# All steps of the block quantization on one engine: the pattern QPAT set from (0, 1, 1, 1, 1, 1, 1, 1) to (1,)

## The chip, the cores and the metric

The kernel runs as one program on the 8 cores of one Trainium2 chip. Each core takes 1024 of the 8192 tokens and works by itself; no data passes between cores. The metric is the device time of the slowest core in microseconds (us). A profile shows one execution on the slowest of its cores; here that is core 5.

The engines are called as in the profile: PE (TensorE, matmul), PEld (its weight load), DVE (VectorE), ACT (ScalarE), POOL (GpSimd), SP (the queue that issues DMAs here).

## The reference, cut to what matters

One transformer layer: linear attention with a memory, a layer norm, and then a feed-forward block whose inputs and weights are quantized in blocks of 32 (a shared power of two per block, and few mantissa bits per element), and a second layer norm. H is 2048, I is 8192.

```python
def _quantize_mx(x, ebits, mfrac, emax_elem, max_norm):
    xb = x.reshape(shp[:-1] + (shp[-1] // BLOCK, BLOCK))
    amax = jnp.max(jnp.abs(xb), axis=-1, keepdims=True)
    sexp = jnp.floor(jnp.log2(jnp.where(amax == 0, 1.0, amax))) - emax_elem
    scale = jnp.exp2(sexp)
    q = _quantize_elem(xb / scale, ebits, mfrac, max_norm) * scale
...
gate = _mx_linear(x, w_gate)
up = _mx_linear(x, w_up)
inter = jax.nn.silu(gate) * up
return _mx_linear(inter, w_down)
```

`_mx_linear` quantizes both operands and multiplies them. The kernel quantizes the float32 weights itself, on every core.

## The kernel before

**Stages.** After the attention (to about 410 us of the span) comes stage C: a layer norm and the quantization of the activations, eight tiles of 128x2048. Then the feed-forward runs over 16 slabs s of 512 columns of I, and a last layer norm ends the kernel.

**Quantizations.** `emit_quant` (L234) is one quantization; outside stage C its tile is 128x1024. It has three parts, and the names are used below.
- *Head*: the product with the inverse scale (L252, `tt`) and the clamp (L254, `ts`), on engine `se`.
- *Middle*: the square on ACT (L255), and then three DVE instructions that build the magic number from it (L256, L257, L259), on DVE whatever `se` is.
- *Tail*: add, subtract and the product with the scale into the bf16 output (L269 to L271), again on `se`, and then `post`, the transposing DMAs issued by SP.

The tail isn't emitted with its own head. It is kept in `tmp["pend"]` and emitted within the next quantization, after that one's head and middle (L263), or by `flushq`. Each engine works in the order in which things were emitted. So an engine that holds consecutive quantizations has the order head q0, (tail of the one before), head q1, tail q0, head q2, tail q1 and so on.

**Which engine.** A counter `QC` runs over all 456 quantizations (8 in stage C, 448 in the slabs). `se` is DVE where `QPAT[k % 8]` is 0, which is every eighth, and POOL elsewhere. The work buffers of the two engines are apart (fy0, fmd0, fmd1 for DVE; fy1, fmd2, fmd3 for POOL). POOL's quantizations alternate over `par`: with `par` 1 the tile y is the borrowed region `yb`, which for weights is `INTER[:, 1024:2048]` and for the intermediate is `WST[:, 1024:2048]` (key `wst0b`).

**A weight job.** `wq_back` (L566) quantizes one pair of staged weight tiles: `emit_search` on DVE (a memset, 15 short chained instructions, a reciprocal that writes `invw`), then four quantizations q0 to q3, each 128x1024. After q1 and after q3 it calls `wq_load_tile` for the next job (L601): two DMAs from ACT's queue into the half of WST just read, and a `tensor_reduce` on DVE for the block maxima. All four quantizations write the one buffer WQN, which a transposing DMA empties each time.

**A slab.** For s above 0 the order is: job d1 of slab s-1 (the second half of w_down), g0 and g1 (w_gate), u0 and u1 (w_up), `down_section(s-1)` (its matmuls and 32 adds to BIG2 on DVE), then four times two gate/up tiles with silu and one quantization of the intermediate (i0 to i3), each with its own search that writes `invi`, and then d0. Pending tails are flushed before the down section, before each of i0 to i3 and before d0. d0's weights are loaded only after i3, since nothing else was in the pipe.

**Where DVE quantizations fall.** A slab has 28 quantizations and the pattern has 8, so it repeats every two slabs. In odd slabs q0 of d1, g1, u1 and d0 is on DVE. In even slabs q0 of g0 and u0, and i0, are on DVE. It is always the first quantization of its job. No two jobs that follow one another without a break are both without a DVE quantization.

Of the kernel before, what the change touches and what calls it, by code (L numbers as in the profile page):

```python
# [161 lines left out]
def build_program():  # L162
# [20 lines left out]
    with ExitStack() as stG:  # L183
# [40 lines left out]
            p.recip(qi_ap, q_ap, [kq], [kqi])  # L224

        QC = [0]
        QPAT = (0, 1, 1, 1, 1, 1, 1, 1)

        def flushq(tmp):
            if tmp["pend"] is not None:  # L230
# [3 lines left out]
        def emit_quant(src_ap, src_keys, inv_bc, scale_tile_ap, blk0, scale_keys,  # L234
                       out_ap, out_keys, kc_col, hi, tmp, tasp, post=()):
            k = QC[0]
            QC[0] += 1
            se = "gp" if QPAT[k % len(QPAT)] else "dve"
            par = tmp["p" + se]
# [536 lines left out]
```

How the kernel before makes its waits and increments, by code:

```python
        def go(h, _w=tuple(waits), _b=build, _hs=hsem, _inc=inc):  # L90
            for hs, v in _w:
                h.wait_ge(hs, v)
            ins = _b(h)
            if _hs is not None:
                ins.then_inc(_hs, _inc)
# [9 lines left out]
    def wait_raw(self, eng, sem, val):  # L105
        hs = self.semh[sem]
        self.ops[eng].append(lambda h, _hs=hs, _v=val: h.wait_ge(_hs, _v))
```

## Time and profile before

| | us |
|---|---|
| median of 2 runs (7924.15 to 7967.17) | 7945.66 |
| the profiled execution | 7966.37 |
| its span on core 5, the slowest | 7964.8 |
| spans of the 8 cores | 7908.4 to 7964.8 |

The profiled execution is 0.26% above the median. All eight cores do the same work within 0.7% of each other. A row of the trace below has the start and the duration in us, the engine, the line, the operation, the tile written and the tiles read, the count, and in square brackets how long the engine had been idle and what ended it. L122, L126, L127, L130, L136, L139 and L144 are the helpers `tt`, `ts` with one scalar, `ts` with two, `stt`, `recip`, `red` and `act`. A reciprocal that writes invw or invi ends a search, so these 160 reciprocals mark the jobs; the stretch from one to the next is called the interval of the job.

### The profile page before, as it was taken

How to read it: one execution, taken by the hardware profiler on the slowest of the kernel's cores; microseconds unless marked ns; L12 is line 12 of the kernel's file. 1: busy time of each engine (PE TensorE's matmuls, PEld its weight loads, DVE VectorE, ACT ScalarE, POOL GpSimd, SP SyncE). 2: the span in 40 equal slices, each digit the busy share in tenths (PEclk: the TensorE clock that was granted, in tenths of full speed). 3: DMA queues.
4: the chain of work that ended last, by engine and by line, in shares of the span. 5: the costliest groups of instructions: out<-in, count | busy, mean ns of one | idle time of the engine just before them, and what ended most of it. 6: DMA issues, size and time to landing. Idle time of an engine off the chain costs nothing.

```text
span 7964.8 us, 37328 instructions; the slowest of 8 cores (7908.4 to 7964.8 us)
## 1 busy us (share of the span) xinstructions
PE 1627.1 (20%) x6816; PEld 712.1 (9%) x6816; DVE 5351.7 (67%) x6206; ACT 596.4 (7%) x634; POOL 4341.0 (55%) x2015
## 2 busy tenths in 40 slices
PE   4400202104040402104040402104040402104041
PEld 2100101001010101001010101001010100001010
DVE  3386666676767666676767666676767667676767
ACT  0010000000000000000000000000000000000001
POOL 0037565574747465574747465574747465564643
PEclk7555656557575756557575756557575756657575
DMA  3001121111212021111212021111212121111111
GB/s 107 0 8 53 27 60 37 53 46 38 57 28 58 24 61 37 48 51 34 62 28 57 25 61 37 48 50 35 61 26 60 25 59 39 48 50 34 56 29 63
DMA packets 670364, 355.00 MB, mean 45 GB/s; under 512 B 499121, under 2 KB 630578, under 8 KB 668978
## 3 DMA queue, kind: packets, MB, share of 16 engines
q10 hardware_dynamic: 169984, 201.35, 8.2%
q1 hardware_dynamic: 496818, 134.49, 7.5%
q0 software_dynamic: 3328, 16.78, 0.6%
q14 instruction: 177, 1.45, 0.1%
q8 instruction: 57, 0.93, 0.0%
HBM read 222.50 MB, written 8.39 MB: 29 GB/s over the span
## 4 chain that ended last, share of the span: by engine, by line
DVE 38%; POOL 27%; issue 13%; PE 10%; DMA 7%; ACT 3%; DVEq 1%; ACTq 1%; POOLq 0%; SPq 0%
POOL fy L122 9%; POOL INTER L122 8%; PE psY L148 7%; DVE s_c L130 7%; POOL WQN L122 5%; DVE fmd L127 4%; DVE fy L122 4%; DVE PSC L139 3%; DVE INTER L127 3%; DMA WST<-wd 3%; DVE scw L122 3%; ACT fmd L144 2%; DVE fmd L130 2%; DVE WQN L122 2%; DVE sci L122 2%
## 5 line engine op out<-in xcount | busy, mean ns | idle before, releaser
L148 PE MATMUL psY<-WDT,INTQF 128*128 128x512 bf16 x2048 | 519.0, 421 | 5445.5 <-DVE BIG L122 2911.8
L127 DVE TENSOR_SCALAR INTER<-fmd 128x1024 f32<-128x1024 f32 x384 | 555.8, 1447 | 1028.0 <-ACT fmd L144 1022.0
L122 POOL TENSOR_TENSOR fy<-fy,fmd 128x1024 f32<-128x1024 f32 x392 | 989.3, 2524 | 328.7 <-DVE fmd L130 290.7
L122 POOL TENSOR_TENSOR INTER<-INTER,fmd 128x1024 f32<-128x1024 f32 x336 | 858.1, 2554 | 200.7 <-DVE fmd L130 167.1
L130 DVE SCALAR_TENSOR_TENSOR fmd<-INTER,smalls,fmd 128x1024 f32<-128x1024 f32 x384 | 891.8, 2322 | 43.8 <-DVE fmd L127 2.3
L127 DVE TENSOR_SCALAR fmd<-fmd,smalls 128x1024 f32<-128x1024 f32 x448 | 806.8, 1801 | 49.1 <-DVE INTER L127 0.9
L148 PEld LDWEIGHTS psY<-WDT,INTQF 128*128 128x128 bf16 x2048 | 215.3, 106 | 5749.3 <-issue 5556.3
L122 POOL TENSOR_TENSOR fy<-WST,invw 128x1024 f32<-128x1024 f32 x168 | 412.5, 2455 | 552.3 <-DVE invw L136 536.6
L122 POOL TENSOR_TENSOR INTER<-WST,invw 128x1024 f32<-128x1024 f32 x168 | 412.5, 2455 | 500.6 <-DVE invw L136 484.9
L139 DVE TENSOR_REDUCE PSC<-WST 128x64 f32<-128x2048 f32 x192 | 438.3, 2283 | 222.4 <-DMA WST<-wd 197.8
L144 ACT ACTIVATE fmd<-fy 128x1024 f32<-128x1024 f32 x252 | 263.8, 1056 | 3611.7 <-POOL fy L127 2269.0
L148 PE MATMUL psG<-WGT,XQF 128*128 128x512 bf16 x1024 | 406.5, 397 | 414.0 <-DVE scw L122 397.9
L148 PE MATMUL psU<-WUT,XQF 128*128 128x512 bf16 x1024 | 407.1, 398 | 187.9 <-DMA WUT<-WQN 108.4
L122 POOL TENSOR_TENSOR WQN<-INTER,scw 128x1024 bf16<-128x1024 f32 x168 | 361.5, 2152 | 121.7 <-DMA WGT<-WQN 33.7
L122 POOL TENSOR_TENSOR WQN<-fy,scw 128x1024 bf16<-128x1024 f32 x168 | 361.5, 2152 | 121.4 <-DMA WGT<-WQN 33.6
L122 DVE TENSOR_TENSOR BIG<-BIG,psY 128x512 f32<-128x512 f32 x512 | 350.0, 687 | 114.6 <-PE psY L148 101.4
L148 PE MATMUL psY<-WGT,XQF 128*128 128x512 bf16 x1024 | 388.1, 379 | 0.0
L148 PE MATMUL psY<-WUT,XQF 128*128 128x512 bf16 x1024 | 388.1, 379 | 0.0
L122 POOL TENSOR_TENSOR WST<-INTER,invi 128x1024 f32<-128x1024 f32 x28 | 53.5, 1911 | 502.5 <-DVE invi L136 502.5
L122 POOL TENSOR_TENSOR fy<-INTER,invi 128x1024 f32<-128x1024 f32 x28 | 53.5, 1911 | 486.0 <-DVE invi L136 486.0
L144 ACT ACTIVATE fmd<-INTER 128x1024 f32<-128x1024 f32 x168 | 177.3, 1055 | 1825.6 <-POOL INTER L127 1825.6
L122 DVE TENSOR_TENSOR scw<-scw,s_c 128x128 f32<-128x128 f32 x480 | 204.8, 427 | 50.7 <-DVE s_c L130 1.2
(170 smaller groups left out, 3895.8 us busy)
## 6 DMA issues: line engine op xcount, KB each, us to landing
WST<-wg ACTq DMA_DIRECT2D x128, 512.0 KB, 4.6
WST<-wu ACTq DMA_DIRECT2D x128, 512.0 KB, 4.7
WST<-wd ACTq DMA_DIRECT2D x128, 512.0 KB, 6.0
xps<-xP POOLq DMA_DIRECT2D x8, 1024.0 KB, 7.0
BIG<-xT SPq DMA_DIRECT2D x16, 512.0 KB, 19.2
y<-BIG POOLq DMA_DIRECT2D x8, 1024.0 KB, 4.2
WGT<-WQN SPq DMA_TRANSPOSE x128, 2.8
WUT<-WQN SPq DMA_TRANSPOSE x128, 2.8
```

What stands on the lines that cost most here:

```text
L122: return self.emit(eng, lambda h: h.tensor_tensor(out, a, b, op), reads, writes)
L127: return self.emit(eng, lambda h: h.tensor_scalar(out, a, s1, s2, op1, op2), reads, writes)
L130: return self.emit(eng, lambda h: h.scalar_tensor_tensor(out, a, s, b, op1, op2), reads, writes)
L139: return self.emit("dve", lambda h: h.tensor_reduce(out, a, AX, op, apply_absolute_value=absval), reads, writes)
L144: return self.emit("act", lambda h: h.activation(out, a, func, bias=bias, scale=scale), reads, writes)
L148: return self.emit("pe", lambda h: h.matmul(out, lhsT, rhs, start=start, stop=stop), reads, writes, quiet=quiet)
```

## The change

The pattern has one entry, 1. `se` is then POOL for all 456 quantizations.

```diff
@@ -224,7 +224,7 @@
         QC = [0]
-        QPAT = (0, 1, 1, 1, 1, 1, 1, 1)
+        QPAT = (1,)
```

What follows in the code: 57 quantizations (one in stage C, 48 of weights, 8 of the intermediate) have head and tail on POOL instead of DVE; their middle stays on DVE and ACT. `par` then alternates over all quantizations, so that i0 and i2 always use the tile fy1 and i1 and i3 always the region `WST[:, 1024:2048]`. No instruction and no DMA is added or removed.

## Rows read from the trace of the kernel before

**Rows 1.** The page, part 1: busy us (share of the span) xinstructions.

```profile
span 7964.8 us, 37328 instructions; the slowest of 8 cores (7908.4 to 7964.8 us)
...
PE 1627.1 (20%) x6816; PEld 712.1 (9%) x6816; DVE 5351.7 (67%) x6206; ACT 596.4 (7%) x634; POOL 4341.0 (55%) x2015
```

**Rows 2.** Instructions by line: xcount | busy us, mean ns | idle before, releasers.

```profile
L122 POOL TENSOR_TENSOR fy<-fy,fmd 128x1024 f32<-128x1024 f32 x392 | 989.3, 2524 | 328.7 <-DVE fmd L130 290.7 <-POOL fy L122 1.3
...
L122 POOL TENSOR_TENSOR WQN<-fy,scw 128x1024 bf16<-128x1024 f32 x168 | 361.5, 2152 | 121.4 <-DMA WGT<-WQN 33.6 <-DMA WDT<-WQN 33.5 <-DMA WUT<-WQN 16.9
...
L122 DVE TENSOR_TENSOR fy<-fy,fmd 128x1024 f32<-128x1024 f32 x112 | 230.1, 2055 | 7.0 <-DVE fy L122 0.5
...
L122 DVE TENSOR_TENSOR WQN<-fy,scw 128x1024 bf16<-128x1024 f32 x48 | 149.3, 3111 | 8.0 <-DVE fy L122 7.1
...
L122 DVE TENSOR_TENSOR fy<-WST,invw 128x1024 f32<-128x1024 f32 x48 | 58.8, 1226 | 5.0
```

**Rows 3.** Busy time by stretch: jobs g1, u0 of slab 1.

```profile
core 5: us, PE busy (x) PEld busy (x) DVE busy (x) ACT busy (x) POOL busy (x), PEclk, DMA share, GB/s
...
1187.73:1236.57 48.84, 0.00 (x0) 0.00 (x0) 39.92 (x38) 4.12 (x4) 26.95 (x12) 0.50 0.20 59
...
1236.57:1296.35 59.78, 0.00 (x0) 0.00 (x0) 41.77 (x33) 4.23 (x4) 49.26 (x23) 0.50 0.21 57
```

**Rows 4.** Sums of that view over 32, 31, 8, 8, 8, 7, 8, 8 intervals.

```profile
sum 1565.32, PE 25.19 PEld 7.96 DVE 1276.66 ACT 131.83 POOL 860.99; mean PE 0.79 PEld 0.25 DVE 39.90 ACT 4.12 POOL 26.91
...
sum 1855.53, PE 65.03 PEld 23.05 DVE 1293.86 ACT 131.11 POOL 1525.84; mean PE 2.10 PEld 0.74 DVE 41.74 ACT 4.23 POOL 49.22
...
sum 390.79, PE 0.00 PEld 0.00 DVE 319.01 ACT 32.95 POOL 215.54; mean PE 0.00 PEld 0.00 DVE 39.88 ACT 4.12 POOL 26.94
...
sum 431.37, PE 0.00 PEld 0.00 DVE 303.23 ACT 33.84 POOL 334.63; mean PE 0.00 PEld 0.00 DVE 37.90 ACT 4.23 POOL 41.83
...
sum 694.99, PE 381.13 PEld 169.47 DVE 454.87 ACT 42.51 POOL 258.49; mean PE 47.64 PEld 21.18 DVE 56.86 ACT 5.31 POOL 32.31
...
sum 674.15, PE 336.88 PEld 149.39 DVE 398.45 ACT 37.97 POOL 344.94; mean PE 48.13 PEld 21.34 DVE 56.92 ACT 5.42 POOL 49.28
...
sum 237.20, PE 0.00 PEld 0.00 DVE 101.81 ACT 8.46 POOL 76.26; mean PE 0.00 PEld 0.00 DVE 12.73 ACT 1.06 POOL 9.53
...
sum 271.35, PE 0.00 PEld 0.00 DVE 101.80 ACT 8.46 POOL 76.27; mean PE 0.00 PEld 0.00 DVE 12.72 ACT 1.06 POOL 9.53
```

**Rows 5.** Timeline: start us, us. From g0's search to g1's in slab 1.

```profile
1118.65 2.28 DVE L139 TENSOR_REDUCE PSC<-WST 128x64 f32<-128x2048 f32 x1
...
1127.95 0.95 DVE L136 RECIPROCAL invw<-scw 128x128 f32<-128x128 f32 x1
...
1129.11 1.91 POOL L122 TENSOR_TENSOR fy<-WST,invw 128x1024 f32<-128x1024 f32 x1 [11.46 <-DVE invw L136]
...
1132.30 5.09 POOL L122 TENSOR_TENSOR INTER<-INTER,fmd 128x1024 f32<-128x1024 f32 x2
...
1175.31 2.28 DVE L139 TENSOR_REDUCE PSC<-WST 128x64 f32<-128x2048 f32 x1
...
1175.53 4.83 POOL L122 TENSOR_TENSOR INTER<-INTER,fmd 128x1024 f32<-128x1024 f32 x2 [1.23 <-DVE fmd L130]
...
1180.62 1.95 DVE L122 TENSOR_TENSOR scw<-scw,s_c 128x128 f32<-128x128 f32 x1
...
1187.73 0.95 DVE L136 RECIPROCAL invw<-scw 128x128 f32<-128x128 f32 x1
```

**Rows 6.** Timeline: after i3 in slab 1 (first two) and slab 3.

```profile
1452.90 1.91 POOL L122 TENSOR_TENSOR INTQ<-WST,sci 128x1024 bf16<-128x1024 f32 x1
...
1460.12 2.29 DVE L139 TENSOR_REDUCE PSC<-WST 128x64 f32<-128x2048 f32 x1 [12.38 <-DMA WST<-wd]
...
2356.27 2.29 DVE L139 TENSOR_REDUCE PSC<-WST 128x64 f32<-128x2048 f32 x1 [7.24 <-DMA WST<-wd]
```

**Rows 7.** Busy time by stretch: one quantization of stage C.

```profile
596.27:618.57 22.30, 0.00 (x0) 0.00 (x0) 14.37 (x4) 1.91 (x1) 21.62 (x6) 0.50 0.10 24
```

## The prediction

> **What bounds the kernel now.** I read the page first, for the shares. DVE is busy 67% of the span, POOL 55%, PE 20% [rows 1]. No engine is near full, so shares can't say what a change is worth; the reader should see only that the two engines between which work moves are the busiest two, and that neither is saturated. So I looked for what ends each job. The timeline of one job shows it [rows 5]: a search writes invw at 1127.95, POOL had been idle 11.46 us and starts at once, and the next search ends at 1187.73. This is a loop. Search, heads and tails on POOL, the middle of q3 on DVE, the block maximum of the next tile (the reduce at 1175.31), search. Each turn waits for the one before, so a job's interval is a piece of the kernel's path, and the time is the sum of intervals plus the attention and the end, which the change doesn't touch.
>
> Next, the busy time by stretch, over one interval of each kind [rows 3]. A job whose q0 is on DVE (DVE-led) takes 48.84 us, one with all four on POOL (all-POOL) takes 59.78. DVE is busy about as long in both (39.92 and 41.77), POOL 26.95 and 49.26. The kernel before thus contains both kinds of every job, and the change turns all of them into the second kind. The sums of that view over all intervals give the prices [rows 4], in the order of the eight rows:
> - 32 DVE-led intervals of d1, g0, g1, u0: 1565.32, mean 48.92. 31 all-POOL ones: 1855.53, mean 59.86.
> - d0, 8 and 8: 390.79 (mean 48.85) and 431.37 (mean 53.92).
> - u1, up to the first search of the intermediate, so with the down section: 8 DVE-led, 694.99 (86.87); 7 all-POOL with a down section, 674.15 (96.31).
> - i3, up to the search of d0: 8 on the tile fy1, 237.20 (29.65); 8 on the region in WST, 271.35 (33.92).
>
> **The change part by part.**
>
> *The moved tail is paid on the path.* On DVE the two adds and the product of a tail take 2 x 2.055 + 3.111 = 7.2 us, on POOL 2 x 2.524 + 2.152 = 7.2 us [rows 2]. So the work isn't dearer on POOL. The matter is where it lies. With q0 on DVE both engines make a head at once and both make tails at once; with q0 on POOL the heads and tails stand in one line between invw and q3's middle. That is the 59.86 - 48.92 = 10.94 us of the two means [rows 4].
>
> *But not all of that stays.* An all-POOL interval in the kernel before is always followed by a DVE-led job (or by a flush). The tail of its q3 is emitted within the next q0, and where this q0 is on DVE no POOL head comes before it. POOL then runs that tail at 1175.53, just as DVE reduces and searches. The search is stretched: a tensor_tensor of 128x128 takes 1.95 us in it [rows 5]. How much, its length tells. From the start of the last reduce to invw it is 1187.73 - 1175.31 = 12.42 us here and 1127.95 - 1118.65 = 9.30 us at the end of the DVE-led job before, where POOL was idle (the 11.46) [rows 5]. The difference is 3.12 us. After the change a POOL head stands ahead of that tail and waits for invw; the tail comes after the search, as at 1132.30, where an all-POOL job already has it and where it is in its 59.86. So an all-POOL job followed by another costs 59.86 - 3.12 = 56.74 us. That isn't shown by any interval of before as a whole; it is put together from two halves that are. Its bounds are 59.86 (nothing saved) and 59.86 - 3.12 - 0.4 (some jobs are 0.35 longer than others, from 59.78 to 60.14, and this could go too).
>
> The Trainium skill has a rule for this stretch (SBUF — State Buffer, "Who interferes with whom"): GpSimd and VectorE share one pair of ports as an exclusive lock, held for a whole instruction, and a VectorE instruction with two SBUF inputs needs it. The stretched tensor_tensor is of that kind, so the trace agrees. By the rule the sum is the one below; without it, if the 3.12 us had another cause, it is that of the first rival.
>
> *The sum over weight jobs.* d1, g0, g1, u0: 63 x 56.74 = 3574.6 against 1565.32 + 1855.53 = 3420.9: +153.7. d0: its all-POOL form has no pending tail at its start and ends in the same stretched search: 53.92 - 3.12 = 50.80, 16 times 812.8 against 822.2: -9.4. u1 is followed by a flush, so its q3 tail stays where it is and nothing is saved: 8 x (96.31 - 86.87) = +75.5. The final d1 is all-POOL already: 0.
>
> *The intermediate.* Eight i0 move to POOL. i0's interval doesn't change by more than 0.2 us between the two kinds; POOL is otherwise idle there. I take 0, with a price of the 10.9 us of a quantization each, 8 x 10.9 = 87 us, if that cover were gone. But the alternation `par` shifts: i3 is then always on the region in WST. There its last instruction on POOL runs from 1452.90, and d0's weights can be loaded into that half of WST only after it, so DVE's reduce waits 12.38 us for the DMA; with the tile fy1 it waits 7.24 [rows 6]. Eight slabs change over: 8 x (33.92 - 29.65) = +34.2. Those are means of eight intervals each [rows 4].
>
> *Stage C.* A steady quantization takes 22.30 us, POOL busy for 21.62 of it [rows 7]. One more on POOL costs at most 22.3. It costs less, since the DVE one ran beside POOL's first one, under contention, and held back POOL's second. Laying the eight out in POOL's order with the steady 22.3 gives about 7. Bounds 0 and 22.3; I take 7, because POOL's idle time at the start of the stage closes.
>
> *DMAs and queues.* No transfer is added. SP's transposes follow each tail as before. WQN, one buffer for all tails, is written every 11.5 us in the all-POOL stretch and was written there at the same pace before.
>
> Sum: 153.7 - 9.4 + 75.5 + 34.2 + 0 + 7 = +261 us. Against the profiled execution's own 7966.4 us that is 8227, +3.3%. That execution is 0.26% above the median of the runs shown; from the median 7945.7 it is 8207 us. That is the forecast.
>
> **The rivals.**
> *A. Nothing is saved.* The stretch of the search is replaced by another of the same size, for instance by q2's tail, if that slips behind the reduce. Then 3.12 us come back 63 + 16 times, +246, in all +507: 8453 us. For it: only the halves were seen. Against: q2's tail ended before the reduce in the DVE-led job, POOL idle for 11.46 us [rows 5].
> *B. DVE is the bound, faster.* DVE is the busiest engine [rows 1], and the change takes 57 heads and tails off it. The Trainium skill says that with VectorE saturated, offloading even to GpSimd may make sense, and in the same place that it might not help, as the two share a port (Perfetto Trace Analysis, "Optimizing Scalar/DVE Operations"). If DVE's work set the time, the tails (7.2 us) and the first product of a head (1.23) [rows 2] would leave: 57 x 8.4 = 479, 7467 us. This decides only if an interval follows DVE's busy time. It doesn't: DVE is busy 1.8 us more in a job that is 10.9 us longer [rows 3], because its instructions stretch beside POOL's.
> *C. Hidden, no change.* POOL is idle 48.84 - 26.95 = 21.9 us in a DVE-led job, and the moved quantization needs 22.3 more (49.26 - 26.95) [rows 3]. If it all fell into that idle time, all jobs would take 48.9 and the change be worth 0 to the old DVE-led jobs: 7946 plus the 41 of i3 and stage C, 7987 us. Against it stand the 31 all-POOL jobs, which have just that load and take 59.86 [rows 4].
>
> **How the numbers follow.** Forecast 0.86, A 0.07, C 0.04, B 0.03. The forecast's own range: without i3's term and with 0.4 us less in 63 jobs it is 8207 - 34 - 25 = 8148; with stage C at 22.3 and half a microsecond more in 79 jobs 8207 + 15 + 40 = 8262, and the runs of before differ by 43 us among themselves. I give 8150 to 8280. It leaves out the rivals, 14 in 100, and a few at its edges. A measurement of this kernel can tell about 2% from no change, 159 us, or 8105 us. The forecast and A are slower by more; C and a thin tail of the forecast are within; B is faster: 0.92, 0.05, 0.03.
>
> **What would show it.** POOL has 57 x 5 = 285 instructions more, 2300, and DVE 285 fewer, 5921. Intervals between invw are near 56.7 for d1, g0, g1, u0, near 50.8 for d0, 96.3 for u1. No 1.95 us tensor_tensor is left in the weights' searches, and 9.3 us lie between the last reduce and invw. i3's interval is near 33.9 in all 16 slabs. DVE's busy time falls by little, some 200 to 300 us, and not by 479. The forecast is wrong if these intervals are 59.8 (A), 49 (C), or if two all-POOL jobs in a row make a wait that none of these halves has, such as the load of the next tile coming late for its reduce.

## The result: 3.2% slower

| | us |
|---|---|
| before, median of 10 runs (7920.26 to 7969.31) | 7956.09 |
| changed, median of 11 runs (8190.33 to 8223.35) | 8194.4 |
| ratio, 95% interval | 1.0322 [1.0300, 1.0344] |
| forecast | 8207 (8150 to 8280) |
| span of the profiled execution, before and changed | 7964.8 and 8190.1 |

**The profile after.** Its part 1, and the first line of the chain that ended last (part 4):

```profile
span 8190.1 us, 37698 instructions; the slowest of 8 cores (8175.6 to 8190.1 us)
...
PE 1628.2 (20%) x6816; PEld 711.8 (9%) x6816; DVE 5110.6 (62%) x5921; ACT 601.1 (7%) x634; POOL 4872.8 (59%) x2300
...
POOL 43%; DVE 26%; issue 14%; PE 10%; DMA 3%; ACT 3%; DVEq 1%; POOLq 1%; ACTq 0%; SPq 0%
```

Against [rows 1], POOL has 285 instructions more and DVE 285 fewer, as counted in the forecast. DVE gives back only 241 us of busy time for them, POOL takes 532 us more, and the span grows by 225. The chain runs over POOL for 43% of the span; before it was DVE that led:

```profile
DVE 38%; POOL 27%; issue 13%; PE 10%; DMA 7%; ACT 3%; DVEq 1%; ACTq 1%; POOLq 0%; SPq 0%
```

The intervals between searches say where the time went. First one weight job, u0 of slab 1 (busy time by stretch; the columns are those of [rows 3]):

```profile
1267.67:1324.28 56.61, 0.00 (x0) 0.00 (x0) 38.60 (x33) 4.23 (x4) 42.67 (x20) 0.50 0.20 56
```

Where [rows 3] had 48.84 and 59.78, all such jobs now take about 56.6 us. The sums of the view, in the order of the four kinds of [rows 4]: 63 intervals of d1, g0, g1, u0; 16 of d0; the 15 of u1 that hold a down section; 16 of i3.

```profile
sum 3566.07, PE 88.24 PEld 30.60 DVE 2424.70 ACT 266.36 POOL 2678.33; mean PE 1.40 PEld 0.49 DVE 38.49 ACT 4.23 POOL 42.51
...
sum 811.60, PE 0.00 PEld 0.00 DVE 557.59 ACT 67.64 POOL 563.33; mean PE 0.00 PEld 0.00 DVE 34.85 ACT 4.23 POOL 35.21
...
sum 1437.74, PE 714.97 PEld 317.50 DVE 854.63 ACT 81.33 POOL 738.90; mean PE 47.66 PEld 21.17 DVE 56.98 ACT 5.42 POOL 49.26
...
sum 517.25, PE 0.00 PEld 0.00 DVE 203.56 ACT 16.90 POOL 152.54; mean PE 0.00 PEld 0.00 DVE 12.72 ACT 1.06 POOL 9.53
```

| intervals | before | forecast | changed, mean | difference in the sum, forecast / found |
|---|---|---|---|---|
| d1, g0, g1, u0 (63) | 48.92 and 59.86 | 56.74 | 56.60 | +153.7 / +145.2 |
| d0 (16) | 48.85 and 53.92 | 50.80 | 50.73 | -9.4 / -10.6 |
| u1 (16, one without a down section) | 86.87 and 96.31 | 96.31 | 95.85 | +75.5 / +70.0 |
| i0, i1, i2 (48) | | no change | 18.95 | 0 / 0 |
| i3 (16) | 29.65 and 33.92 | 33.92 | 32.33 | +34.2 / +8.6 |
| up to the first weight search | | | | +7 / +11.0 |
| the last down section and layer norm | | 0 | | 0 / +0.8 |

The last column adds up to +261 forecast and +225 found between the two profiled spans. (The found +70.0 of u1 counts its first interval too, 79.96 and 81.37 us.) Only i3 is far from its term. Why it is, the last experiments show.

Now the piece that no interval of before had shown as a whole, the search between two all-POOL jobs. Timeline of the end of that job and the start of the next: POOL, then DVE.

```profile
1306.63 5.09 POOL L122 TENSOR_TENSOR fy<-fy,fmd 128x1024 f32<-128x1024 f32 x2
...
1311.87 2.17 POOL L122 TENSOR_TENSOR WQN<-fy,scw 128x1024 bf16<-128x1024 f32 x1
...
1325.44 1.91 POOL L122 TENSOR_TENSOR fy<-WST,invw 128x1024 f32<-128x1024 f32 x1 [11.40 <-DVE invw L136]
...
1315.04 2.28 DVE L139 TENSOR_REDUCE PSC<-WST 128x64 f32<-128x2048 f32 x1
...
1318.42 0.29 DVE L130 SCALAR_TENSOR_TENSOR s_c<-s_c,scw 128x128 f32<-128x128 f32 x1
...
1318.82 0.29 DVE L122 TENSOR_TENSOR scw<-scw,s_c 128x128 f32<-128x128 f32 x1
...
1324.28 0.95 DVE L136 RECIPROCAL invw<-scw 128x128 f32<-128x128 f32 x1
```

POOL finishes the tail of q2 at 1314.04 (1311.87 + 2.17) and then has nothing that doesn't need invw: it is idle 11.40 us. So the reduce at 1315.04 and the whole search have no POOL instruction beside them. The two search instructions shown take 0.29 us, where [rows 5] had 1.95 for the second of them, and from the reduce to invw it is 1324.28 - 1315.04 = 9.24 us (9.30 was put in, 12.42 is the stretched form).

### The profile page after: what moved, and what is told of

It is laid out like the page before. It is cut to its first block, busy times and chain, and to the rows that moved or that the text cites. A ratio compares the mean times of both kernels' runs of the same rounds, so it can differ in the third digit from the quotient of the medians.

```text
span 8190.1 us, 37698 instructions; the slowest of 8 cores (8175.6 to 8190.1 us)
## 1 busy us (share of the span) xinstructions
PE 1628.2 (20%) x6816; PEld 711.8 (9%) x6816; DVE 5110.6 (62%) x5921; ACT 601.1 (7%) x634; POOL 4872.8 (59%) x2300
## 4 chain that ended last, share of the span: by engine, by line
POOL 43%; DVE 26%; issue 14%; PE 10%; DMA 3%; ACT 3%; DVEq 1%; POOLq 1%; ACTq 0%; SPq 0%
POOL INTER L122 17%; POOL fy L122 12%; POOL WQN L122 7%; PE psY L148 7%; DVE s_c L130 6%; DVE fmd L127 4%; DVE PSC L139 3%; ACT fmd L144 2%; DVE INTER L127 2%; DVE sci L122 2%; DVE scw L122 2%; POOL fy L127 2%; POOL WST L122 2%; DMA WST<-wd 2%; POOL INTER L127 1%
## 5 line engine op out<-in xcount | busy, mean ns | idle before, releaser
L127 DVE TENSOR_SCALAR INTER<-fmd 128x1024 f32<-128x1024 f32 x384 | 615.5, 1603 | 1466.3 <-ACT fmd L144 1464.1
L122 POOL TENSOR_TENSOR fy<-fy,fmd 128x1024 f32<-128x1024 f32 x448 | 1107.5, 2472 | 225.2 <-DVE fmd L130 178.4
L127 DVE TENSOR_SCALAR fmd<-fmd,smalls 128x1024 f32<-128x1024 f32 x448 | 1037.5, 2316 | 50.2 <-DVE INTER L127 2.3
L130 DVE SCALAR_TENSOR_TENSOR fmd<-INTER,smalls,fmd 128x1024 f32<-128x1024 f32 x384 | 1033.2, 2691 | 43.0 <-DVE fmd L127 1.4
L122 POOL TENSOR_TENSOR INTER<-INTER,fmd 128x1024 f32<-128x1024 f32 x384 | 945.0, 2461 | 63.0 <-DVE fmd L130 20.8
L122 POOL TENSOR_TENSOR INTER<-WST,invw 128x1024 f32<-128x1024 f32 x192 | 505.5, 2633 | 27.0 <-POOL WQN L122 0.9
L144 ACT ACTIVATE fmd<-fy 128x1024 f32<-128x1024 f32 x224 | 236.7, 1057 | 3710.0 <-POOL fy L127 3710.0
L122 POOL TENSOR_TENSOR WQN<-fy,scw 128x1024 bf16<-128x1024 f32 x192 | 425.4, 2216 | 28.1 <-POOL fy L122 0.9
L122 POOL TENSOR_TENSOR WQN<-INTER,scw 128x1024 bf16<-128x1024 f32 x192 | 412.4, 2148 | 28.1 <-POOL INTER L122 0.9
L127 POOL TENSOR_SCALAR fy<-fy 128x1024 f32<-128x1024 f32 x224 | 232.8, 1039 | 36.5 <-POOL fy L122 36.5
```

The costliest lines, as they stand in the source:

```text
L122: return self.emit(eng, lambda h: h.tensor_tensor(out, a, b, op), reads, writes)
L127: return self.emit(eng, lambda h: h.tensor_scalar(out, a, s1, s2, op1, op2), reads, writes)
L130: return self.emit(eng, lambda h: h.scalar_tensor_tensor(out, a, s, b, op1, op2), reads, writes)
L144: return self.emit("act", lambda h: h.activation(out, a, func, bias=bias, scale=scale), reads, writes)
```

## The experiments

Each is compared with the kernel before on the same chip; the ratios are those of runs to runs of before. The kernel before took 7927.7 us on the chip of the first four experiments and 7931.5 on that of the next four (medians of 7), against 7956.1 above, so a difference in us between two sections is uncertain by some 30 us; the intervals are not. The intervals are read as above, on the slowest core of each run.

### Does i3's load wait for the tile? Yes

The edit swaps the two tiles for the intermediate; `W`, the width, is only computed further up (those lines are left out here).

```diff
...
-            if se == "gp" and par == 1 and yb is not None:
+            if se == "gp" and par == (0 if kc_col == 6 and W == 1024 else 1) and yb is not None:
                 y, kys = yb, list(yb_keys)
             else:
-                y, kys = tmp["y"][se], [ky + str(par if se == "gp" else 0)]
+                y, kys = tmp["y"][se], [ky + "0"]
```

> The changed kernel, with the two work tiles swapped for the intermediate: i1 and i3 use the tile fy1, i0 and i2 the region WST[:, 1024:2048]. Theory (d0's load waits for i3's last POOL instruction because that one reads the half of WST to be loaded): the 16 intervals of i3, 32.3 us in the changed kernel, go to the 29.7 that slabs with the tile fy1 had in the kernel before, so 16 x 2.6 = 42 us less than the changed kernel's 8194, about 8152, and DVE's first wait for the wd load there falls from 11.9 to about 7.2 us. Rival (the wait is the transfer itself, whatever the tile): i3 stays at 32.3 and the time at 8194.

Measured 8111.6 us, ratio 1.0223 [1.0199, 1.0247]: 1.0 point below the changed kernel's 1.0322, about 80 us, of which the 16 i3 intervals hold 86 (517.25 - 430.81). First the changed kernel after i3 of slab 1 (timeline: POOL's last instruction of i3, DVE's reduce), then DVE's reduce after i3 of slab 7 in this run, and the sum over its 16 i3 intervals:

```profile
1489.75 1.91 POOL L122 TENSOR_TENSOR INTQ<-WST,sci 128x1024 bf16<-128x1024 f32 x1
...
1496.44 2.29 DVE L139 TENSOR_REDUCE PSC<-WST 128x64 f32<-128x2048 f32 x1 [11.86 <-DMA WST<-wd]
```

```profile
4236.82 2.29 DVE L139 TENSOR_REDUCE PSC<-WST 128x64 f32<-128x2048 f32 x1 [6.03 <-DMA WST<-wd]
...
sum 430.81, PE 0.00 PEld 0.00 DVE 203.62 ACT 16.90 POOL 152.56; mean PE 0.00 PEld 0.00 DVE 12.73 ACT 1.06 POOL 9.53
```

The mechanism holds: with i3 on fy1 the wait falls from about 12 us to 5.7 to 6.7 in 12 of the 16 slabs (7.1 to 8.5 in slabs 0 to 3), and the interval from 32.33 to 26.93. The size was expected at half of what it is: the expectation took 29.65 for the tile fy1 from [rows 4], and it is 26.93 here. The last experiments say why.

### Same work, another order: the loop sets the time

```diff
                     if nxt is not None:
+                        if idx == 1:
+                            flushq(tmpw)
                         wq_load_tile(nxt[0], nxt[1], nxt[2] + idx, nxt[3])
```

> The changed kernel (all on POOL), with the tail of q3 emitted at the end of its own job, ahead of the next job's first head, instead of behind it. The work of each engine stays the same, to the instruction. Theory (the loop from invw to invw sets the time, and a search with a POOL tail beside it is stretched by 3.1 us): a job then has no pending tail at its start but a stretched search at its end, the form that d0 had in the kernel before, 53.9 us. So 63 intervals of d1, g0, g1, u0 go from 56.7 to 53.9 (-176), 16 of d0 from 50.7 to 53.9 (+51), 15 of u1 from 95.9 to about 90 (-89): about 7980 us. Rival (POOL's total work, or its rate, sets the time, not the place of its work): no change, 8194.

Measured 7999.5 us, ratio 1.0084 [1.0060, 1.0107], 195 us less than the changed kernel with the same number of instructions on every engine. The sum of the 63 job intervals, and the end of one job (POOL's tail of q3, DVE's reduce and invw):

```profile
sum 3398.52, PE 93.17 PEld 31.44 DVE 2394.28 ACT 266.34 POOL 2633.01; mean PE 1.48 PEld 0.50 DVE 38.00 ACT 4.23 POOL 41.79
...
2143.76 4.83 POOL L122 TENSOR_TENSOR INTER<-INTER,fmd 128x1024 f32<-128x1024 f32 x2 [1.23 <-DVE fmd L130]
...
2143.53 2.28 DVE L139 TENSOR_REDUCE PSC<-WST 128x64 f32<-128x2048 f32 x1
...
2155.95 0.95 DVE L136 RECIPROCAL invw<-scw 128x128 f32<-128x128 f32 x1
```

The mean is 3398.52 / 63 = 53.94 us, the expected form. POOL's tail of q3 lies beside the search again, and from reduce to invw it is 2155.95 - 2143.53 = 12.42 us, the stretched length to the hundredth. It pays all the same: 3.1 us of stretch against 5.9 us (59.86 - 53.92 of [rows 4]) of tail that no longer stands between invw and q3. POOL's amount of work doesn't set the time; what stands in the loop does. The 20 us over the expectation are i3 again: 34.16 us on the profiled core and its neighbour, 32.2 on the six others, whose spans are 7963 to 7971 us against 7997 and 7998.

### The same split between the engines, another place

```diff
-        QPAT = (0, 1, 1, 1, 1, 1, 1, 1)
+        QPAT = (1, 1, 1, 0, 1, 1, 1, 1)
```

> The kernel before with the one DVE quantization in eight put last in its job (q3) instead of first: pattern (1,1,1,0,1,1,1,1). The split of the work between DVE and POOL is that of the kernel before. Rival (the balance of work between the two engines decides): 7956 as before. Theory (the place in the loop decides): a DVE q3 takes head and middle in DVE's own queue, behind the middle of q2, so the search begins hardly earlier; its tail delays the next job's q1 and the buffer WQN. I expect intervals of about 55 to 56 us for both kinds of job instead of 48.9 and 59.9, mean 1.1 more than before, about 8030 us (7990 to 8080).

Measured 8015.7 us, ratio 1.0104 [1.0081, 1.0128]: slower than before with the same split of the work. The sum over the 63 intervals, and DVE in one job whose q3 it holds (invw, head, last instruction of the middle, reduce):

```profile
sum 3472.80, PE 84.38 PEld 29.37 DVE 2475.75 ACT 266.34 POOL 2359.20; mean PE 1.34 PEld 0.47 DVE 39.30 ACT 4.23 POOL 37.45
...
2097.85 0.95 DVE L136 RECIPROCAL invw<-scw 128x128 f32<-128x128 f32 x1
...
2133.68 1.21 DVE L122 TENSOR_TENSOR fy<-WST,invw 128x1024 f32<-128x1024 f32 x1
...
2142.81 1.28 DVE L130 SCALAR_TENSOR_TENSOR fmd<-INTER,smalls,fmd 128x1024 f32<-128x1024 f32 x1
...
2144.01 2.29 DVE L139 TENSOR_REDUCE PSC<-WST 128x64 f32<-128x2048 f32 x1
```

The mean is 55.12 us against 54.30 in the kernel before (3420.9 / 63), and the intervals are near 54.8 and 55.4, not 48.9 and 59.9. DVE begins q3's head only behind q2's middle (2133.68), so the reduce stands at the same distance from invw as in an all-POOL job, within 2 us (2144.01 - 2097.85 = 46.2; 47.4 in [rows 5]). The expectation had the place right and the size within 15 us. Not all of the kernel follows it: on the slowest core u1 takes 82 us more in all than in the kernel before and i3 69 us less (part of that a disturbance of i3 in before, see the last experiments), which nearly cancel.

### The opposite of the change

```diff
-        QPAT = (0, 1, 1, 1, 1, 1, 1, 1)
+        QPAT = (0, 1, 1, 1)
```

> The opposite of the change: pattern (0,1,1,1), q0 of every weight job (and of every i0, and two of stage C) on DVE. Theory: each DVE-led job is now followed by another, whose q3 tail runs beside the search, so its interval is 48.9 + 3.1 = 52.0 us: 63 x 52.0 against 63 x 56.7 in the changed kernel (-296), d0 52.0 against 50.7 (+20), u1 86.9 against 95.9 (-144), stage C and i3 about -30 together: about 7740 us, 2.7% faster than the kernel before. Rival (DVE is the scarce engine, and the kernel before had the best split): 7956 or slower. Rival 2 (contention for the shared port grows with more on both engines): intervals well above 52.

Measured 7714.9 us, ratio 0.9728 [0.9701, 0.9756], faster than both kernels. Sum of the 63 intervals, and one search (DVE; then the POOL tail beside it):

```profile
sum 3282.23, PE 84.57 PEld 30.13 DVE 2710.61 ACT 259.34 POOL 2111.53; mean PE 1.34 PEld 0.48 DVE 43.03 ACT 4.12 POOL 33.52
...
1153.29 2.28 DVE L139 TENSOR_REDUCE PSC<-WST 128x64 f32<-128x2048 f32 x1
...
1156.27 0.29 DVE L130 SCALAR_TENSOR_TENSOR s_c<-scw,PSC 128x128 f32<-128x128 f32 x1
...
1156.67 1.82 DVE L130 SCALAR_TENSOR_TENSOR s_c<-s_c,scw 128x128 f32<-128x128 f32 x1
...
1158.59 1.95 DVE L122 TENSOR_TENSOR scw<-scw,s_c 128x128 f32<-128x128 f32 x1
...
1166.06 0.95 DVE L136 RECIPROCAL invw<-scw 128x128 f32<-128x128 f32 x1
...
1153.51 4.83 POOL L122 TENSOR_TENSOR INTER<-INTER,fmd 128x1024 f32<-128x1024 f32 x2 [1.23 <-DVE fmd L130]
```

The mean is 52.10 us. DVE is busier than in any kernel so far, 43.0 of those 52 us, and the time falls: the rival that DVE is the scarce engine (B of the forecast) is out. What is added to the 48.9 is the stretch of the search, 1.82 and 1.95 us for two instructions while POOL's tail runs, 1166.06 - 1153.29 = 12.77 us from reduce to invw. The instruction just before them, beside the same tail, has one input in SBUF (scw) and one in PSUM, writes the same SBUF tile, and takes 0.29 us; none of the 480 of its kind exceeds 0.29 us in this trace or in that of before.

### What stretches the search

```diff
-            s_c2 = sf("s_c2", [128, 128])
...
-            PSC = pf("PSC", [128, 160])
+            PSC = pf("PSC", [128, 288])
+            s_c2 = PSC[:, 160:288]
...
```

The same edit on the changed kernel (the control, where no POOL work lies beside the weights' searches) and on the kernel with every job DVE-led.

> The changed kernel with one edit: the searches' scratch s_c2 lies in PSUM (behind PSC, in the same bank) instead of SBUF, so that none of the 15 search instructions has two SBUF inputs. This is the control for the next run. Theory (a search instruction with two SBUF inputs waits for POOL's): in the weights' searches of the changed kernel nothing is stretched, so its intervals of 56.7, 50.7 and 95.9 stay; the searches of i1, i2, i3 do have POOL's tail beside them (1.5 and 1.95 us instead of 0.19) and lose up to 3.1 us each, 48 of them, less what PE then bounds: 8194 - 70 to 150, about 8090 us. A price of PSUM access would show as longer instructions in the weights' searches; the ones that read PSC take 0.29 us as the others do, so I expect none. Rival (the stretch has another cause): 8194 and i1 to i3 still 18.9.

> Every job DVE-led (pattern (0,1,1,1)), and the searches' scratch in PSUM. Here POOL's q3 tail lies beside every weight search. Theory: the 3.1 us of each go, 52.0 becomes 48.9: 63 + 16 times 3.1 = -245, and i1 to i3 another -70 to -150 as in the control: 7715 - 245 - 100 = about 7370 us. Rival (the stretch is no matter of the second SBUF input): 7715 less only what the control shows.

The control measured 8062.9 us, ratio 1.0163 [1.0139, 1.0186]. Its 63 job intervals, and its 48 of i0, i1, i2:

```profile
sum 3569.04, PE 88.07 PEld 30.49 DVE 2427.15 ACT 266.51 POOL 2677.77; mean PE 1.40 PEld 0.48 DVE 38.53 ACT 4.23 POOL 42.50
...
sum 764.45, PE 551.93 PEld 242.19 DVE 433.88 ACT 102.76 POOL 458.78; mean PE 11.50 PEld 5.05 DVE 9.04 ACT 2.14 POOL 9.56
```

The weights' intervals stay (56.65, were 56.60), and those of the intermediate go from 18.95 to 15.93 us. The DVE-led kernel measured 7385.8 us, ratio 0.9304 [0.9283, 0.9325]. Its 63 intervals, and a search with the POOL tail beside it:

```profile
sum 3086.95, PE 88.26 PEld 30.57 DVE 2515.18 ACT 259.34 POOL 2108.82; mean PE 1.40 PEld 0.49 DVE 39.92 ACT 4.12 POOL 33.47
...
1135.79 2.28 DVE L139 TENSOR_REDUCE PSC<-WST 128x64 f32<-128x2048 f32 x1
...
1139.18 0.30 DVE L130 SCALAR_TENSOR_TENSOR PSC<-PSC,scw 128x128 f32<-128x128 f32 x1
...
1139.58 0.29 DVE L122 TENSOR_TENSOR scw<-scw,PSC 128x128 f32<-128x128 f32 x1
...
1145.44 0.95 DVE L136 RECIPROCAL invw<-scw 128x128 f32<-128x128 f32 x1
...
1136.01 4.83 POOL L122 TENSOR_TENSOR INTER<-INTER,fmd 128x1024 f32<-128x1024 f32 x2 [1.23 <-DVE fmd L130]
```

The mean is 49.00 us instead of 52.10. The tail on POOL runs as before, right beside, and the same two instructions take 0.30 and 0.29 us. So the stretch needs two things at once, POOL instructions beside the search and search instructions whose two inputs both lie in SBUF; taking away either one removes it. The edit also moves the scratch that those instructions write, but writing to SBUF is not what stretches: `s_c<-scw,PSC` of the section before writes there and stays at 0.29 us. The Trainium skill says that a VectorE instruction with two SBUF inputs contends with a GpSimd instruction that reads SBUF, and one with at most one SBUF input, outside the 2-port perf modes, does not (SBUF — State Buffer, "Who interferes with whom"); both halves agree with these traces. Writing to PSUM costs 0.01 us per instruction.

### All together, and the other side of the optimum

The first: weight jobs DVE-led, i0 to i3 on POOL with i1 and i3 on fy1, scratch in PSUM. The part of the edit that chooses the engine (the tiles and the scratch are changed as above):

```diff
...
-            QC[0] += 1
-            se = "gp" if QPAT[k % len(QPAT)] else "dve"
+            if not (kc_col == 6 and W == 1024):
+                QC[0] += 1
+            se = "dve" if k % 4 == 0 and not (kc_col == 6 and W == 1024) else "gp"
```

> All together: weight jobs DVE-led, all of i0 to i3 on POOL with i1 and i3 on the tile fy1, the searches' scratch in PSUM. Theory: against the run before, i3 goes from a mean of 29.3 (half of the slabs near 32, half near 26.4) to 26.4 in all slabs, -46 us, and i0 stays: about 7320 us. Rival (an i0 on POOL without other cover costs its 10.9 us): 7320 + 175.

Measured 7282.3 us, ratio 0.9176 [0.9156, 0.9196], 8% less than the kernel before. Its 16 i3 intervals sum to

```profile
sum 427.84, PE 0.00 PEld 0.00 DVE 204.49 ACT 16.90 POOL 152.54; mean PE 0.00 PEld 0.00 DVE 12.78 ACT 1.06 POOL 9.53
```

26.74 us each. It is 38 us better than expected because i0 on POOL doesn't just cost nothing: with the search no longer stretched an i0 on POOL takes 15.97 us and one on DVE 18.85 (the run before). The rival's 10.9 us each are out.

The second keeps the searches as they were and puts two quantizations of each job on DVE, `QPAT = (0, 1, 0, 1)`.

> Pattern (0,1,0,1): q0 and q2 of each job on DVE, searches as in the kernel before. One more head and tail go from POOL to DVE. Theory: in a DVE-led job DVE is already busy 40 of 49 to 52 us, and five more instructions of 10.4 us in all don't fit: DVE becomes the engine that sets the interval, 54 to 58 us: about 8000 us (7850 to 8150), so the other side of the optimum. Rival (the more that runs side by side the better, POOL being the slow one): intervals below 52 and a time below 7715.

Measured 7757.0 us, ratio 0.9790 [0.9751, 0.9830]. The 63 intervals:

```profile
sum 3268.17, PE 88.28 PEld 30.63 DVE 2860.28 ACT 259.49 POOL 1529.56; mean PE 1.40 PEld 0.49 DVE 45.40 ACT 4.12 POOL 24.28
```

51.88 us, no more than with one (52.10). My expectation of 54 to 58 was wrong: DVE's other instructions get shorter as POOL has less to run beside them (the three of the middle from 18.7 to 11.9 us a job in all), so DVE is busy only 2.4 us longer (45.4). The rival had the direction right by 0.2 us and the time wrong: the kernel as a whole is 42 us slower than with one, by u1 (+26) and by i3 (+50), less 34 in other places. i3's tile is the WST region in every slab with this pattern. With none, one in eight, one in four and one in two on DVE the kernel takes 8194, 7956, 7715 and 7757 us.

### Why i3's term was off

Two more runs, one execution each. The first is the changed kernel with w_down loaded in long rows; it loads another piece of w_down of the same size, so its product is another one. (The lines that issue the two DMAs change with it and are left out here.) The second is the kernel before, unchanged.

```diff
-                    srcap = wd.rearrange("(c p) i -> p c i", p=128)[
-                        :, :, s * ISLAB + ti * 128: s * ISLAB + (ti + 1) * 128]
+                    n4 = s * NQT + ti
+                    srcap = wd[(n4 // 4) * 128:(n4 // 4 + 1) * 128,
+                               (n4 % 4) * 2048:(n4 % 4 + 1) * 2048]
...
```

> The changed kernel with w_down's tiles loaded in rows of 4 KB (a different piece of w_down of the same size) instead of in pieces of 512 bytes; the product with w_down is then of the wrong weights, all work stays the same. Theory (what differs between cores in i3 is the landing of the load in small pieces, which a neighbour core's load at the same moment slows): the load lands like that of w_gate and w_up (4.4 instead of 4.9 us), i3 goes from 32.1 us to about 31, and cores whose pair starts i3 within 2 us of them show no 34. Rival (any load is slowed by a neighbour's, or the pieces don't matter): 32.1, and 34 where a pair is close.

> The kernel before, unchanged, for a second trace of it. Theory (two cores of a pair, 0 and 1, 2 and 3, 4 and 5, 6 and 7, slow each other's w_down load when they reach i3 within 2 us of each other): every pair with a larger offset has i3 at 26.2 (tile fy1) and 32.0 (region in WST) and 7058 to 7066 us between the first and the last weight search; a pair that is closer has 29.6 and 34.0 and about 45 us more. Rival (cores 4 and 5 are slower by themselves): they have 29.6 and 34.0 whatever their offset.

Measured 8222.9 and 7936.6 us. Of the first only the i3 intervals on core 4 are used: cores 0 to 3 took 8181 to 8221 us at a granted clock of 0.586 to 0.589, cores 4 to 7 took 8162 to 8171 at 0.595 to 0.596.

All eight cores are in each trace. The times of a core count from its own first instruction, and no view has a clock common to two cores. So the distances below, between the starts of the i3 intervals of two cores, take it that a pair starts together; that they sort the intervals as they do speaks for it. In the profiled execution of before, cores 4 and 5 reached i3 within 2 us of one another in every slab; the other pairs were 3 to 12 us apart. The sums of eight i3 intervals each, on fy1 and on the WST region, on core 0 of that same execution, against 237.20 and 271.35 on core 5 in [rows 4]:

```profile
sum 208.99, PE 0.00 PEld 0.00 DVE 101.78 ACT 8.45 POOL 76.32; mean PE 0.00 PEld 0.00 DVE 12.72 ACT 1.06 POOL 9.54
...
sum 255.93, PE 0.00 PEld 0.00 DVE 101.77 ACT 8.45 POOL 76.32; mean PE 0.00 PEld 0.00 DVE 12.72 ACT 1.06 POOL 9.54
```

26.1 and 32.0 us, against 29.65 and 33.92. From the first to the last weight search it is 7056 to 7066 us on six cores, and 7109 and 7110 on cores 4 and 5. In the second trace of before, core 5 was 5 to 9 us from core 4, and its sums are

```profile
sum 207.54, PE 0.00 PEld 0.00 DVE 101.81 ACT 8.45 POOL 76.27; mean PE 0.00 PEld 0.00 DVE 12.73 ACT 1.06 POOL 9.53
...
sum 256.40, PE 0.00 PEld 0.00 DVE 101.78 ACT 8.45 POOL 76.27; mean PE 0.00 PEld 0.00 DVE 12.72 ACT 1.06 POOL 9.53
```

with 7061 us from first to last search: nothing is slow about core 5 itself. There cores 2 and 3 were 0.7 to 1.4 us apart in slabs 0 to 4 and 4 to 7 us from slab 5 on. Their i3 took 28.6 to 31.2 and 34.0 to 34.6 us in the first five slabs and 25.7 to 26.7 and 31.9 to 32.8 in the rest; from first to last search 7078 and 7081. Over nine of the traces (before, changed, and all runs but the one with q3 on DVE and the last two), four pairs and 16 slabs each:

| distance of the pair at i3, us | i3 on fy1: count, mean | i3 on the WST region: count, mean |
|---|---|---|
| under 1 | 10, 30.7 | 6, 35.2 |
| 1 to 2 | 16, 29.3 | 74, 34.2 |
| 2 to 3 | 12, 28.2 | 8, 33.6 |
| 3 to 4 | 18, 27.5 | 68, 32.4 |
| 4 and more | 392, 26.2 | 548, 32.2 |

The rival of a slow core falls. The spans of executions without a kept trace show the pairs too. Of the 12 executions of the changed kernel with all spans on record, 7 took 8190 to 8194 us; in each of the 5 that took 8216 to 8223, both cores of one or two pairs took 8214 to 8222 and all others 8194 or less. In the kernel before, in each of the 6 of 17 that took over 7940 us, the two longest cores (in one of them the four longest) are whole pairs. What is not shown is the cause as such: no run sets the distance on purpose, so "close together" and "long i3" are seen to go together and to end together, and no more.

The forecast's i3 term took both its numbers from a disturbed core and was set against a changed kernel whose pairs were all 3.5 us or more apart. From the first to the last weight search all its cores take 7317 to 7324 us, 251 to 268 more than the six. In i3 alone the rise between undisturbed cores is 16 x 32.2 - 208.99 - 255.93 = +50 us, and between the profiled ones +8.6 (517.25 - 508.55), since in the profiled execution of the changed kernel no pair was close. With w_down in long rows the loads land in 4.3 us instead of 4.9 (medians over the kernel; 6.0 on core 5 of before), and the 16 i3 intervals on core 4 are

```profile
sum 502.84, PE 0.00 PEld 0.00 DVE 203.61 ACT 16.90 POOL 152.53; mean PE 0.00 PEld 0.00 DVE 12.73 ACT 1.06 POOL 9.53
```

31.43 us instead of 32.2: the small pieces cost 0.8 us of an undisturbed i3. No pair came within 2 us in this run, so whether long rows would end the disturbance is open, and so is what the two cores share. The Trainium skill says that the two cores of a domain share the HBM's bandwidth (HBM Reference, "Specifications (TRN2)"); that fits pairs 0 and 1, 2 and 3 and so on, and no run here tells it from another shared part.

## Why the prediction was right, step by step

- **What bounds the kernel.** The loop from invw to invw: right. Moving one tail out of it, with no change in work, gave 195 us; DVE at its highest share gave a faster kernel.
- **The search unstretched, 3.12 us.** Right, and it was the step that mattered. The 59.86 us of the all-POOL jobs of before became 56.60; taking the long form over as it stood would have given rival A's 8453. The cause of the stretch was shown apart, by the scratch in PSUM on the DVE-led kernel.
- **d1, g0, g1, u0: +153.7, found +145.2.** The mean of 62 of them is 56.70. What I missed is slab 0's g0: it has no pending tail and takes 50.69, as d0 does, so 6 us of the 8.5.
- **d0: -9.4, found -10.6; u1: +75.5, found +70.0.** Right. u1's intervals alternate between about 95.4 and 96.5 us in the changed kernel, which is not explained.
- **i0 at nothing: right. i3: +34.2, found +8.6.** The mechanism is right; the term was mis-sized, since both rows it was read from held 2 to 3.5 us that go with a neighbour close by. Between undisturbed cores it is +50. The sign given for it, 33.9 us in all 16 slabs, failed: it is 32.33. The step that failed is reading a price off one core without looking at the others: the spans of before, 7908 to 7965 us for the same work, were the sign, and [rows 4] was read on the slowest of them.
- **Stage C: +7, found +8.1.** From the reciprocal before the stage to the first weight search, before and changed (busy time by stretch):

```profile
503.32:701.30 197.98, 0.00 (x0) 0.00 (x0) 132.33 (x50) 15.18 (x8) 153.63 (x35) 0.50 0.13 32
...
506.21:712.28 206.07, 0.00 (x0) 0.00 (x0) 119.85 (x45) 15.28 (x8) 168.66 (x40) 0.50 0.12 31
```

  The other 2.9 us came before the stage, in the attention, which the change doesn't touch.
- **What would show it.** 2300 and 5921 instructions, DVE's busy time down by 241 us (200 to 300 was said), no long search instruction, 9.24 us from reduce to invw: as written. i3's interval was not, as said.
- **The rivals.** A (8453), B (7467) and C (7987) are each out by more than 200 us. C's idle time on POOL is real, 11.40 us in the job shown of the changed kernel, and the moved work can't use it, because the head that would fill it needs invw. The flush puts a tail there, and gains.

The forecast of 8207 was 13 us over the median. Part of that is luck. Against the profiled spans i3 was 25 us too high and the jobs 15, stage C and the attention 4 too low. Between the executions that by their times no pair disturbs (before, the four of ten at 7920 to 7926 us; changed, the six of eleven at 8190 to 8194) the change costs 268 us, near the +261 of the sum, with i3 16 us too low there. But the starting point, 7946, lay between such executions and disturbed ones, and so does the median of before, 7956, while the changed kernel's 8194 does not: the medians differ by 238.

## What to carry to other kernels

Where two engines take turns around a dependent loop, as here, neither's busy share prices a move between them. Find the event that closes the loop, take the interval of each kind of turn, and put the new kind together from halves that the trace already has, with the seam between two such turns looked at by itself. Where a chain of small VectorE instructions runs beside GpSimd work, try to give each at most one input in SBUF: here a scratch tile moved to PSUM was worth 330 us of 7715 (131 of the changed kernel's 8194, where only the searches of i1 to i3 had POOL beside them). And an idle stretch is only of use to work that doesn't wait for what ends it.

## What the runs showed of the hardware that I had not expected

- Where two cores of a pair reach i3, and with it the load of w_down, within 2 us of one another, the interval of both is 2 to 4 us longer each time (table), and they can stay together for the whole kernel: about 45 us, 0.6%. The executions of before spread by 49 us, and where the spans of all cores are on record the long ones are whole pairs; that it is i3 in each of them is shown only where there is a trace.
- A 128x128 DVE instruction that reads and writes PSUM takes 0.30 us, one that writes SBUF 0.29.
- A second DVE quantization in a job gives DVE 10 us of instructions more, but only 2.4 us of busy time, since the three instructions of the four middles take 11.9 us instead of 18.7 when POOL has 24 us of work in the job instead of 33.5.
